# A fused attention block on one core: later outputs, a shared batch seam and a reordered last loop

## What is computed

```
xn = layernorm(x) * ln_w + ln_b
q = softmax(xn @ Wq + bq, within a head);  k = softmax(xn @ Wk + bk + mask, over the tokens)
v = (xn @ Wv + bv) * mask
att = k^T v per head;  y = q att
h = silu(layernorm(y) * (1 + scale) + shift)      # scale, shift from silu(cond) @ W_emb
out = x + h @ W_out + b_out
```

## Time and profile before

| | us |
|---|---|
| median of 3 runs (lowest, highest) | 556.83 (555.85, 561.12) |
| profiled execution, its own time | 560.96 |
| its span, first to last instruction | 559.1 |
| PE busy | 486.9 (87%) |
| DVE busy | 372.9 (67%) |
| ACT busy | 260.8 (47%) |
| POOL busy | 127.4 (23%) |

### The profile page before, as it was taken

One profiled execution on the slowest core, in us unless ns is written; L12 is line 12 of the kernel. 1 busy time (PEld: TensorE's weight loads), 2 busy tenths in 40 slices (PEclk: granted clock), 3 DMA queues, 4 the chain that ended last, 5 costly groups with the idle time before them and its releaser, 6 DMA issues.

```text
span 559.1 us, 7116 instructions
## 1 busy us (share of the span) xinstructions
PE 486.9 (87%) x2414; PEld 383.8 (69%) x2414; DVE 372.9 (67%) x847; ACT 260.8 (47%) x475; POOL 127.4 (23%) x106
## 2 busy tenths in 40 slices
PE   3889999998999999989989999779999557877666
PEld 1568777866866878878878877557778446666444
DVE  6578868768678288987787667548773756475522
ACT  3424332416564233654645564655651265666460
POOL 0013311212000011332423342440000032444342
PEclk9989999999999999999999999789999978999799
DMA  7981111112232110011321321233200001222232
GB/s 265 324 316 38 39 38 39 38 39 95 76 112 63 50 39 23 17 57 39 113 76 39 114 76 39 75 112 116 76 0 1 0 1 63 89 75 81 70 113 75
DMA packets 23075, 43.48 MB, mean 78 GB/s; under 512 B 1976, under 2 KB 2048, under 8 KB 23040
## 3 DMA queue, kind: packets, MB, share of 16 engines
q1 hardware_dynamic: 21712, 40.41, 21.6%
q10 hardware_dynamic: 1328, 2.62, 1.3%
HBM read 34.64 MB, written 8.39 MB: 77 GB/s over the span
## 4 chain that ended last, share of the span: by engine, by line
PE 64%; DVE 15%; issue 8%; ACT 8%; POOL 3%; DMA 2%; ACTq 0%; POOLq 0%; DVEq 0%
PE ps L902 17%; PE ps L903 16%; PE ps L904 16%; PE ps L907 6%; PE ps L1048 3%; ACT y L322 2%; DVE th L724 2%; DMA y<-in_L_cond_Wk_dram 2%; PE ps L995 1%; POOL res L484 1%; ACT u L334 1%; ACT eqT L245 1%; PE ps L1032 1%; PE ps L949 1%; DVE zT_lo L588 1%
## 5 line engine op out<-in xcount | busy, mean ns | idle before, releaser
L473 POOL TENSOR_TENSOR qs<-qs,qmax 128x512 f32<-128x512 f32 x32 | 36.0, 1124 | 273.1 <-DVE qmax L614 273.1
L334 ACT ACTIVATE u<-ps,ab 128x128 f32<-128x128 f32 x128 | 48.2, 457 | 32.9 <-PE ps L907 27.5
L902 PE MATMUL ps<-wq_hi,zT_hi 128*128 128x512 f32 x128 | 52.6, 411 | 1.9 <-DVE qs L609 1.9
L902 PE MATMUL ps<-wk_hi,zT_hi 128*128 128x512 f32 x128 | 53.2, 416 | 1.0 <-DVE kf L595 1.0
L902 PE MATMUL ps<-ek_hi,zm_hi 128*128 128x512 f32 x128 | 51.1, 399 | 2.2 <-DVE ek_lo L650 1.1
L724 DVE SCALAR_TENSOR_TENSOR th<-th,u 128x512 f32<-128x512 f32 x32 | 24.2, 757 | 42.9 <-ACT th L337 42.9
L903 PE MATMUL ps<-wq_lo,zT_hi 128*128 128x512 f32 x128 | 51.2, 400 | 0.0
L904 PE MATMUL ps<-wq_hi,zT_lo 128*128 128x512 f32 x128 | 51.2, 400 | 0.0
L484 POOL TENSOR_TENSOR res<-res,bo_all 128x512 f32<-128x512 f32 x32 | 44.9, 1404 | 26.7 <-DMA res<-in_x_dram 26.7
L907 PE MATMUL ps<-ident,y 128*128 128x128 f32 x128 | 21.8, 296 | 33.4 <-ACT y L322 33.4
L904 PE MATMUL ps<-wk_hi,zT_lo 128*128 128x512 f32 x128 | 50.6, 395 | 0.0
(11 more groups left out here) (149 smaller groups left out, 1134.2 us busy)
## 6 DMA issues: line engine op xcount, KB each, us to landing
x_in<-in_x_dram SPq DMA_DIRECT2D x31, 512.0 KB, 3.6
res<-in_x_dram SPq DMA_DIRECT2D x32, 256.0 KB, 2.8
out_dram<-res SPq DMA_DIRECT2D x32, 256.0 KB, 2.0
y<-in_L_cond_Wk_dram ACTq DMA_DIRECT2D x1, 1024.0 KB, 8.7
kf<-in_L_cond_Wq_dram ACTq DMA_DIRECT2D x1, 1024.0 KB, 11.8
eq<-in_L_cond_W_out_dram SPq DMA_DIRECT2D x1, 1024.0 KB, 7.6
wv_mod<-in_L_cond_Wv_dram SPq DMA_DIRECT2D x1, 1024.0 KB, 9.8
eq<-in_L_cond_W_emb_dram SPq DMA_DIRECT2D x4, 256.0 KB, 10.4
```

The source lines that it names most:

```text
L334: act.activation(blk(u, f), blk(ps[:, YTB, :], f), ACT.Identity, bias=ab[:, m // T, 1, f:f + 1], scale=ab[:, m // T, 0, f:f + 1]).then_inc ...
L473: pool.tensor_tensor(q_heads, q_heads, qmax[:].unsqueeze(2).broadcast_to([P, H, DH]), ALU.subtract).then_inc(s["q_shift"], 1)
L902: pe.matmul(o, a[0], bb[0], start=start, stop=False)
```

## The change

- Outputs. For tiles from HT = 12 on, u, th, the split h and the PSUM bank alternate between two places (`u_of`, `th_of`, `h_hi`, `h_lo`, `o_bank`), and `scale_shift` waits for the tile before the last instead of the last one.
- Last loop. `turn_y` of output tile j stands at step NS[j], `product_out` at step NS[j]+2 and `out_tile` at NS[j]+3, with NS = 2, 3, 4, 5, 7, 8, ..., 18. In a step PE does the product before `turn_y`; ScalarE does `scale_shift` first and `h_high` last. The statistics of y come in groups of 2, 2, 3, 3, 3, 3 tiles.
- Batch 0's end. Outputs 11 to 13 stand between `product_q(1, 15)`, `product_g(1, 0)` and `product_g(1, 1)`, output 14 behind `turn_q(16)`, and 15 in step 1 of the last loop. `turn_kmax(1)` stands ahead of `product_out(10)`.
- `k_less_max` reads the spread maximum in PSUM; `keys_max` is gone.
- The sums of exponentials stand once, behind a state's last `product_g`; after batch 0's, the condition's columns, `turn_z(1, 0)`, `products_att(0)` and `turn_q(0)` follow.
- Odd tiles from 3 on are masked by ScalarE (an activation with scale and bias ahead of the split).
- Start. Wk comes in two halves ahead of x tiles 2 and 3, which wait for its second half; its splits and `key_bias` go by halves; x's first statistics are of 2 and 2 tiles; `product_q(0, 1)` has a bank of its own, so it no longer waits for `q_add(0, 0)`.

```
-    XC = [[(0, 4), (4, 8), (8, 12), (12, 16)]] * 2
-    YC = [[(0, 4), (4, 8), (8, 12), (12, 16)], [(0, 2), (2, 4), (4, 8), (8, 12), (12, 16)]]
+    XC = [[(0, 2), (2, 4), (4, 8), (8, 12), (12, 16)]] * 2
+    YC = [[(0, 4), (4, 8), (8, 12), (12, 14), (14, 16)], [(0, 2), (2, 4), (4, 7), (7, 10), (10, 13), (13, 16)]]
...
+    NS = [2, 3, 4, 5] + [n + 3 for n in range(4, 16)]
+    HT = 12
...
-            return (zm_hi, ek_hi)[m % 2][:, HI - 1, :]
+            return (zm_hi, ek_hi)[m % 2][:, HI - 1, :] if m < HT else zT_hi[:, m % 2].rearrange("p f c -> p (f c)")
...
+        def u_of(m):
+            return u[:] if m < HT or m % 2 == 0 else y[:, 4, :] if m < T else kf[:, 0, :]
+        def th_of(m):
+            return th[:] if m < HT or m % 2 == 0 else y[:, 5, :] if m < T else kf[:, 1, :]
+        def o_bank(m):
+            return ps[:, OB if m < HT or (m > HT + 2 and m % 2) else ZB, :]
+        def masked_by_act(n):
+            return n >= 3 and n % 2 == 1
...
-            act.dma_start(x_in[:, 2:4, :], x_tok[:, 2:4, :]).then_inc(x_pair[1], 16)
-            for w, raw, done in ((wk, wk_raw, "wk_in"), (wq, wq_raw, "wq_in")):
-                act.dma_start(raw, w.rearrange("(c p) n -> p c n", p=P)).then_inc(s[done], 16)
+            for v, at in ((ln_w, LNW), (ln_b, LNB)):
+                act.dma_start(ln_rows[at:at + NB, :], v.rearrange("(c p) -> c p", p=P)).then_inc(s["ln_in"], 16)
+            for half in range(2):
+                act.dma_start(wk_raw[:, 2 * half:2 * half + 2, :],
+                              wk.rearrange("(c p) n -> p c n", p=P)[:, 2 * half:2 * half + 2, :]).then_inc(s[f"wk_in{half}"], 16)
+            act.dma_start(wq_raw, wq.rearrange("(c p) n -> p c n", p=P)).then_inc(s["wq_in"], 16)
...
+                if masked_by_act(n):
+                    act.wait_ge(landed, value)
+                    act.wait_ge(s["xm_ok"], 2 * nth_chunk(XC, b, n))
+                    act.activation(x_in[:, at, :], x_in[:, at, :], ACT.Identity, bias=xm_shift[:, n:n + 1],
+                                   scale=xm_r[:, n:n + 1]).then_inc(s["zm_act"], 1)
+                    act.wait_ge(s["zm_act"], nth_masked(b, n, True))
+                else:
+                    act.wait_ge(s["zm_ok"], nth_masked(b, n, False))
                 place_free(b, n)
...
-                    act.wait_ge(s["h_lo_ok"], m)
+                    act.wait_ge(s["h_ok"], m if m <= HT else m - 1)
...
-                    act.activation(blk(u, f), blk(ps[:, YTB, :], f), ACT.Identity, bias=ab[:, m // T, 1, f:f + 1],
+                    act.activation(blk(u_of(m), f), blk(ps[:, YTB, :], f), ACT.Identity, bias=ab[:, m // T, 1, f:f + 1],
...
+                if m:
+                    act.wait_ge(s["h_lo_ok"], m if m <= HT else m - 1)
+                act.activation(th_of(m), u_of(m), ACT.Tanh).then_inc(s["th_ok"], 1)
...
-                if m >= 2:
+                if m in (HT, HT + 1):
+                    act.wait_ge(s["q_ps"], 2 * T + m - HT - 1)
+                elif m >= 2:
...
                     turned_q(t + 1)
                 if 1 <= t <= T - 2:
                     exp_q(1, t - 1)
+                if t >= NT:
+                    normalise_y(t - NT)
+                if t == T - 1:
+                    normalise_y(HT)
                 if t + 2 < T:
                     normalise_x(1, t + 2)
                 if t >= NT:
-                    normalise_y(t - NT)
                     scale_shift(t - NT)
...
-            normalise_y(T - 4)
-            h_high(T - 5)
-            normalise_y(T - 3)
-            scale_shift(T - 4)
-            normalise_y(T - 2)
-            normalise_y(T - 1)
+            h_high(HT - 1)
             zm_high(1, 0)
-            zm_high(1, 1)
-            h_high(T - 4)
-            scale_shift(T - 3)
-            keys_max(1)
-            exp_q(1, T - 2)
-            h_high(T - 3)
-            scale_shift(T - 2)
+            normalise_y(HT + 1)
             exp_k(1, 0)
             ek_high(1, 0)
-            h_high(T - 2)
-            scale_shift(T - 1)
+            scale_shift(HT)
+            zm_high(1, 1)
             exp_k(1, 1)
             ek_high(1, 1)
-            h_high(T - 1)
-            state_steps(1)
+            h_high(HT)
+            scale_shift(HT + 1)
+            exp_q(1, T - 2)
+            normalise_y(HT + 2)
+            def last_outputs(n):
+                if n < 3:
+                    h_high(HT + 1 + n)
+                if n < 2:
+                    scale_shift(HT + 2 + n)
+                if n == 0:
+                    normalise_y(HT + 3)
+                if n == 2:
+                    exp_q(1, T - 1)
+            state_steps(1, last_outputs)
+            sums_out(1)
             turned_q(T)
-            for i in range(T + 6):
-                m = T + i
-                if 0 <= i - 5 < T:
-                    h_high(m - 5)
+            for i in range(NS[-1] + 2):
+                if i - 1 in NS:
+                    scale_shift(T + NS.index(i - 1))
                 if i + 1 < T:
-                    turned_q(m + 1)
-                if i == 1:
-                    exp_q(1, T - 1)
-                if 0 <= i - 4 < T:
-                    normalise_y(m - 4)
-                    scale_shift(m - 4)
+                    turned_q(T + i + 1)
+                if i in NS:
+                    normalise_y(T + NS.index(i))
+                if i - 1 in NS:
+                    h_high(T + NS.index(i - 1))
         @block.gpsimd
...
-            q_shift(1, T - 1)
+                if m < HT + 1:
+                    q_shift(1, m + 3)
...
-                dve.wait_ge(s["kmax_ok"], b + 1)
-                dve.tensor_tensor(kf[:, n, :], kf[:, n, :], km[:], ALU.subtract).then_inc(s["k_shift"], 1)
+                dve.wait_ge(s["kmax_ps"], b + 1)
...
-                    att_blocks(0)
...
             keys_top(1)
-            out_tile(T - 6)
+            y_raw(T - 1)
+            masked_z(1, 0)
+            silu(HT - 1)
+            out_tile(HT - 2)
+            k_less_max(1, 0)
+            zm_low(1, 0)
+            k_less_max(1, 1)
+            ek_low(1, 0)
+            masked_z(1, 1)
             q_add(1, T - 2)
             q_top(1, T - 2)
-            masked_z(1, 0)
-            masked_z(1, 1)
-            silu(T - 4)
-            out_tile(T - 5)
-            k_less_max(1, 0)
-            zm_low(1, 0)
-            silu(T - 3)
-            out_tile(T - 4)
-            k_less_max(1, 1)
-            silu(T - 2)
-            out_tile(T - 3)
-            ek_low(1, 0)
-            masked_z(1, 2)
-            k_less_max(1, 2)
-            silu(T - 1)
-            out_tile(T - 2)
...
+            k_less_max(1, 2)
+            masked_z(1, 2)
+            def last_outputs(n):
+                if n in (1, 2):
+                    out_tile(HT + n - 1)
+                if n < 3:
+                    silu(HT + 1 + n)
+            state_steps(1, last_outputs)
             att_blocks(1)
-            for i in range(T + 7):
-                m = T + i
-                if 0 <= i - 5 < T:
-                    silu(m - 5)
-                if 0 <= i - 7 < T:
-                    out_tile(m - 7)
+            out_tile(HT + 2)
+            for i in range(NS[-1] + 4):
+                if i - 3 in NS:
+                    out_tile(T + NS.index(i - 3))
+                if i == 2:
+                    out_tile(HT + 3)
                 if i < T:
-                    y_tile(m)
-                    y_stats(m)
+                    y_tile(T + i)
+                if i - 1 in NS:
+                    silu(T + NS.index(i - 1))
+                if i < T:
+                    y_raw(T + i)
+                    y_finish(T + i)
...
-                    pe.wait_ge(s["k_sum"], m)
+                    pe.wait_ge(s["k_sum"], m if m > 2 else 1)
...
+                if m >= 2:
+                    pe.wait_ge(s["q_sum"], m if m > 2 else 1)
...
-            def sum_exponentials(b, n):
-                pe.wait_ge(s["k_exp"], T * b + n + 1)
-                for k in range(4):
-                    pe.matmul(ps[32 * k:32 * k + 32, YB, :], ones[:], kf[:, n - 3 + k, :], start=(n == 3), stop=(n == T - 1))
+            def sum_exponentials():
+                for r in range(0, T, 4):
+                    for k in range(4):
+                        last = pe.matmul(ps[32 * k:32 * k + 32, YB, :], ones[:], kf[:, r + k, :], start=(r == 0), stop=(r == T - 4))
+                last.then_inc(s["den_sum"], 1)
...
-                    pe.wait_ge(s["o_ok"], m)
-                if m == T:
+                    pe.wait_ge(s["o_ok"], m if m < HT + 3 else m - 1)
+                if m == HT + 3:
                     pe.wait_ge(s["gT_d"], 4)
...
+            pe.wait_ge(s["cols_ok"], 1)
+            pe.wait_ge(s["wk_in0"], 16)
+            key_bias(0)
+            key_bias(1)
+            turn_z(0, 0)
             pe.wait_ge(s["vec_in"], 5 * 16)
             turn(ps[:, YB + 1, 0:ROWS - FIRST], vec_rows).then_inc(s["vec_ps"], 1)
-            pe.wait_ge(s["cols_ok"], 1)
```

(61 more changed lines are left out.)

244 lines of the change are left out of this document (135 added, 109 removed).

## The result

| | before | after |
|---|---|---|
| median (lowest to highest), us | 556.48 (555.85 to 561.12), 4 runs | 517.79 (516.58 to 521.33), 4 runs |
| profiled execution: own time, span | 560.96, 559.1 | 521.33, 519.5 |
| mean granted clock | 0.969 | 0.984 |
| PE, DVE, ACT, POOL busy | 486.9, 372.9, 260.8, 127.4 | 476.5, 376.8, 267.6, 128.2 |

The ratio is 0.9304, 95% interval 0.9245 to 0.9362: 7.0% less time. The forecast was 513 with a range of 502 to 529; the median is 4.8 us above it. Of the 39.6 us by which the span is shorter, 10.4 are busy time of PE (a matmul at the low clock counts as busy for longer) and the rest is idle time of PE.

The account below looks back on a forecast made before the run. PE was taken as the bound, losing time where it idles or runs at the low clock, in the seam and last loop. 559.1 - 10.1 - 22.3 - 6.1 = 520.6, less 5.8 gives 514.8 span, median 513 us; range 502 to 529.

Parts of the forecast that it names:

- The steady steps: Last loop, steps 9 to 15: taken as 5.1 us each, between bounds of 4.75 and 5.6; seven make 35.7 us.
- The seam's two new waits: Seam: turn_kmax ahead of product_out(10), taken as 2 us; first state product's second pair of blocks, taken as 1.
- signs of being wrong: Steps near 6, small VectorE instructions over 1 us, h_low releasing outputs, PE idle in early state steps, batch 0 no earlier.
- the first rival: Last loop: VectorE and GpSimd meetings decide, steps at 5.6 to 6.1, 521 us; chance 0.27 together with the second rival.
- The last loop: From turn_q(16) to the end: 126.5 us before, 104.2 forecast with outputs 14 and 15 inside, a gain of 22.3.
- the 3 set for the clock: Last loop: 3 us added for low-clock stretches, as early steps and tail still idle; bounds 0 and 6.
- The seam: Batch 0's end to the second state: 13.1 us of waits and low clock removed, less 3 of new waits, gain 10.1.
- The second rival: Seam's wait only moves: ScalarE slips in the state steps, 8 us, 521; chance 0.27 together with the first rival.
- The loop of stage 4: Stage 4: x_finish moves behind the queries' work, gain 1 us, bounds -2 and 3.
- Batch 0's first half: Keys' maximum read in PSUM takes a copy out of a chain: gain 0.5 us, bounds -0.5 and 1.5.
- Slow clock throughout: Third rival: PE at the low clock for the whole last loop, some 35 us, 548; chance 0.04.
- slower than before: Fourth rival: every last-loop step pays the whole chain, 9.0 us instead of 5.1, 55 us more, 568; chance 0.02.

Follow-up runs that it names:

- Experiment 1: Changed kernel with the last loop alone put back to its old order, outputs 14 and 15 still moved: 540.81 us, ratio 0.9649 to the kernel before.
- experiment 3: Changed kernel with turn_y ahead of product_out again in each last-loop step on PE: 532.68 us, ratio 0.9518 to the kernel before.
- experiment 2: Changed kernel with one u and one th for the second batch's outputs, list order as changed: 518.61 us, ratio 0.9258 to the kernel before.
- experiment 6: Changed kernel with h_low of the second batch's outputs on VectorE, GpSimd keeping add_bias: 514.56 us, ratio 0.9192 to the kernel before.
- experiment 11: Changed kernel without the output bias addition in the second batch, so part of the computation is missing: 513.31 us, ratio 0.9167 to the kernel before.
- experiment 5: The changed kernel run again unchanged, also called its repetition: 517.12 us, ratio 0.9245 to the kernel before.
- 12: Changed kernel with x of tiles 2 and 3 loaded at once, not behind Wk's second half: 518.41 us, ratio 0.9259 to the kernel before.
- 7: Changed kernel with turn_kmax and spread_kmax later on TensorE, query additions of tiles 14 and 15 earlier on VectorE: 522.05 us, ratio 0.9326.
- 10: Changed kernel with only the query additions of tiles 14 and 15 earlier on VectorE, TensorE's order as changed: 523.74 us, ratio 0.9354.
- 9: Changed kernel with only turn_kmax behind output 10 and its spread behind tile 14's query product on TensorE: 519.64 us, ratio 0.9279.

## Why the prediction was right, and where it missed

**Right.** The reading of the last loop held: PE was idle because a turn that was not ready stood ahead of an output that was. Experiment 1 puts 16 us or more on the loop's lists, experiment 3 over half of it on that exchange alone, experiment 2 nothing on the places of u and th. The steady steps were forecast at 5.1 us and take 5.2 (452.57 to 489.00 for seven). The seam's two new waits were given 2 and 1 us and show 1.99 and 1.32.

**Right by luck.** `turn_q(16)` was forecast near 410 and stands at 410.46, but four of the five stretches before it miss by 1 to 3 us and cancel. The factor from a profiled execution to the median, 0.9926, came out again (517.79 to 521.33 is 0.9932) only because both profiled executions were of the kind with the lower clock; in experiments 1 and 6 the profiled one was the fastest of its kernel.

**Its own signs.** Of the signs of being wrong, three are there in part: every third steady step lasts near 6 us (6.12 and 6.11; the others 4.1 to 5.4), small VectorE instructions take over 1 us, and the low part releases outputs seven times (7.0 us). They belong to the first rival, whose effect is real and small.

**The last loop, 104.2 forecast, 109.0 measured.** By the forecast's own marks from `turn_q(16)`: step 1 ends at 9.7 (forecast 9.7), step 8 at 42.1 (40.7), step 15 at 78.5 (76.4, with 36.4 instead of 35.7 for the steady steps), and the rest takes 30.5 us against 24.8. These marks are 1.4, 0.7 and 5.7 us over the forecast, 7.8 in all, of which the 3 set for the clock cover a part. The clock was undersized: 13 us at 0.87 and 6 at 0.50 cost about 1.7 + 3.0 = 4.7 (an estimate; the bounds were 0 and 6), 1.7 more than was set. Most of it is in the tail: from 497.12 to 502.40 one output's 12 matmuls take 5.28 us instead of 2.89. The other 3.1 us are 0.7 in the steady steps, 1.0 in the last store, which took 3.5 us instead of 2.5, and the rest in the tail's waits, for which the forecast's steps of 4.8 and 4.25 us had left 1.5 and 0.95 over PE's own 3.3.

**The meetings (first rival).** Its mechanism is there: five of the last loop's six chains have two held-up links, at back-to-back `h_low` and `add_bias`. Its price was not: 5.2 us per step instead of 5.6 to 6.1. My forecast took 5.1 as the middle between no meeting and two; both steady chains had two, so its bound of 5.6 was the case that applied, and that 5.1 fits is partly luck. What was wrong is the slip of 2.7 us for each such chain: its two held-up links add 1.9, and the seven steady steps, with two chains, lie 3.2 us above seven times 4.75, or 1.6 per chain. In those seven steps experiment 11 has two meetings less and gains 2.1 us, experiment 6 three less and gains 2.6: about 1 us each. By the medians the two gain 3.8 and 2.6 us; the 6.1 to 7.3 us between the profiled last loops contain the clock of the execution and the store as well. Experiment 6 also makes the low part itself shorter (0.69 us instead of 1.27), so 11 is the cleaner of the two. Two of the forecast's sums here don't come out: eleven steps at 0.5 to 1.0 us more are 5.5 to 11 us, not 7 to 9, and the chances of an end within 1% add up to 0.04, not 0.03.

**The seam, 10.1 forecast, 8.1 measured** (13.9 less the 5.8 of outputs 14 and 15). The forecast credited all of the idle and slow time, less two new waits of 3 us. What it left out is the clock: 330 to 362 still runs at 0.95, which is 1.6 us by that number. The traces bear it out: from tile 5's turn to the sums of the state, experiments 3 and 11, whose seam has the same code and happened to run at 1.00, take 354.4 us, and the changed kernel, its repetition and experiments 1, 2, 6 and 12, with the same code at 0.95, take 355.8 to 356.0. The second rival, ScalarE slipping in the state steps, didn't come: the only further wait for an output is 0.23 us. Experiments 7 and 10 show how near it was: with the chain 5.7 and 7.1 us later ScalarE waits 5.06 us in both, and the state ends 3.0 and 5.4 us later.

**The loop of stage 4, 1 forecast, 4.3 measured**, outside its bounds of -2 and 3. In the windows PE is busy 138.99 of 144 us before (197 to 341) and 138.61 of 140 after (193 to 333): the same work with 5.0 and 1.4 us idle. The waits for the normalised y there fell from 4.5 us in 4 to 1.4 in 1. I had costed only the moved `x_finish`; that `normalise_y` moved ahead of `normalise_x` on ScalarE, and that the y statistics' groups and the masks on ScalarE change VectorE's list as well, was not laid out. Which of them carries the 3.3 us was not tried, so this gain is not explained.

**Batch 0's first half, 0.5 forecast, -1.5 measured.** The turn of the maximum stands at 122.15 against 123.37, so of the 2.8 us won at the start 1.6 are lost again before it. They are lost at once: from tile 4's turn to tile 5's it is 7.64 us (38.90 to 46.54) against 6.08 (41.74 to 47.82), and from there on the two kernels keep step. Tile 4's turn now follows a wait of 3.86 us, and 38 to 42 runs at a clock of 0.61, its matmuls at 0.63 us instead of 0.39. The forecast knew that tile 4 waits for its statistics, but not the clock behind that wait. From the turn of the maximum to the first state product it is 6.73 against 6.85, so reading the maximum in PSUM gave 0.1, not 0.5: the issue wait of 0.89 and the wait of 1.11 for the second split were left, as the forecast said of the latter.

**Slow clock throughout, and slower than before:** neither shows. From 414 to 516 the clock is 0.95 on the mean, and a closed loop would take 9.0 us per step where 5.2 are measured.

## What to carry to other kernels

When an in-order engine waits for a chain, look first at what is ready right behind the waiting instruction and exchange the two: here that one exchange was worth 10 to 15 us, and a second place for u and th nothing. Before moving a small operation ahead to take away a visible wait, write down what the operation itself waits for and everything queued behind it on its engine and on the next: a wait of 1.3 us removed cost 5.4. And where a serial chain of tiny VectorE instructions can fall beside GpSimd, count the GpSimd instructions that run back to back there: here each held up one link to its end. And when PE has waited, look at the granted clock behind the wait: it cost 1.6 us at the start, 1.5 in the seam and about 4.7 in the last loop.

## What the hardware showed that was not expected

- Three kinds of VectorE links with a single SBUF input were held up by GpSimd (L592, up to 1.05; L594, 1.23; L596, 1.21 us, at 0.17 alone), of 128x2 to 128x4 elements. In the prediction I had named only instructions with two SBUF inputs. The same page of the Trainium skill ("SBUF — State Buffer", "Who interferes with whom") counts `tensor_scalar` among the operations that can enter a mode with both ports and then contend with GpSimd; the trace agrees in that they are held up, even at two to four elements per partition (the mode itself isn't in a trace). The batch-norm instructions were not held up. In the changed kernel's timeline a statistics instruction and an aggregation begin inside a GpSimd instruction and take their usual time (the 32 statistics of y take 0.68 to 0.70 us):

```profile
195.54 0.69 DVE L575 BATCH_NORM_STATS2 yst_raw<-y 128x6 f32<-128x512 f32 x1
...
347.23 0.18 DVE L590 BATCH_NORM_AGGREGATE yst_mv<-yst_raw 128x2 f32<-128x6 f32 x1
```
```profile
194.81 1.05 POOL L528 TENSOR_TENSOR qs<-qs,qmax 128x512 f32<-128x512 f32 x1 [62.16 <-DVE qmax L673]
...
347.10 1.30 POOL L535 TENSOR_TENSOR zT_lo<-th,zT_hi 128x512 fp32r<-128x512 f32 x1 [0.36 <-ACT zT_hi L274]
```

- Of two GpSimd instructions back to back, both held up a link: the held link of 489.38 ended at 490.42, when the second GpSimd instruction had begun, and the next link was then held to that one's end.
- One kernel's executions lie 4.5 to 6.0 us apart (515.58 to 520.12 in experiment 5, 517.19 to 523.17 in 9), and in the changed kernel the granted clock of the execution goes with it (0.993 to 0.997 below 516.1, 0.983 and 0.984 from 518.2 on); the first use of Wk alone moves by 1.65 us between kernels with the same start.
- The low clock follows PE's idle time also here: 0.61 over 4 us from 38 on, around the end of the wait of 3.86 us; 6 us at 0.50 whose start lies in the second of two waits, 1.24 and 1.71 us; and with the low parts on VectorE the low stretch is earlier and costs less (489 to 495 at 0.72).
